# An audio tower on one core: a new order of the same stages on every engine

## The reference

```python
h = layernorm(patches @ tok_W.T + tok_b) * gamma + beta
# attention 0: 16 heads of 64, causal, tanh-capped scores, gated
q, k, v = (layernorm(h) @ w_qkv) split by heads
attn = softmax(causal(50 * tanh(q @ k.T / 8 / 50)))
h = h + ((attn @ v) * sigmoid(layernorm(h) @ w_gates)) @ w_out
# feed-forward 0: three products, then tanh
h = h + tanh(layernorm(h) @ weight @ aux1 @ aux2 + bias)
# attention 1: 16 heads of 16, a sparse (Fenwick) mask
h = h + (softmax(mask(q1 @ k1.T / 4)) @ v1) @ W_proj + b_proj
# feed-forward 1: inputs and weights rounded to blockwise FP4 first
y = fp4(layernorm(h))
h = h + fp4(silu(y @ fp4(w_gate).T) * (y @ fp4(w_up).T)) @ fp4(w_down).T
```

## Time and profile before

| | |
|---|---|
| three runs | 325.51, 326.44, 325.51 us; median 325.51 |
| profiled execution | span 326.4 us, from its first to its last instruction |
| TensorE (matmuls) busy | 303.4 us, 93%, 5142 matmuls |
| VectorE busy | 240.5 us, 74%, 519 instructions |
| ScalarE busy | 121.4 us, 37% |
| mean granted clock of TensorE | 0.989 of 2.4 GHz |

### The profile page before, as it was taken

How to read it: one execution, slowest core, us unless ns; L and a number is a source line. 1 busy time by engine, 2 the same in 40 slices (tenths; PEclk the granted TensorE clock), 3 DMA queues, 4 the chain that set the end, 5 groups by cost and what they waited for, 6 DMA issues and landing times.

```text
span 326.4 us, 11811 instructions
## 1 busy us (share of the span) xinstructions
PE 303.4 (93%) x5142; PEld 265.7 (81%) x5142; DVE 240.5 (74%) x519; ACT 121.4 (37%) x267; POOL 26.1 (8%) x50
## 2 busy tenths in 40 slices
...
DMA packets 8821, 12.80 MB, mean 39 GB/s; under 512 B 826, under 2 KB 5698, under 8 KB 8772
## 3 DMA queue, kind: packets, MB, share of 16 engines
q1 hardware_dynamic: 8772, 12.06, 11.2%
...
## 4 chain that ended last, share of the span: by engine, by line
PE 81%; DVE 10%; DMA 3%; issue 3%; ACT 1%; SPq 1%; POOL 0%; DVEq 0%; ACTq 0%
PE psum L1226 71%; PE psum L1416 2%; DMA ffw_raw<-in_L_ffn_aux_weight_dram 2%; PE psum L1542 2%; PE psum L1438 1%; DMA tokw_raw<-in_L_tok_W_dram 1%; PE psum L1297 1%; PE psum L1322 1%; DVE qs L846 1%; DVE hha L849 1%; DVE qma L1174 1%; PE psum L1253 1%; PE psum L1345 1%; ACT qma L759 1%; PE psum L1519 1%
## 5 line engine op out<-in xcount | busy, mean ns | idle before, releaser
L555 POOL TENSOR_TENSOR ln_rs<-ln_mv,minus_half 128x1 f32<-128x1 f32 x40 | 24.9, 628 | 262.4 <-DVE ln_mv L917 262.4
L1226 PE MATMUL psum<-aT_hi,wqkv_hi 128*128 128x256 f32 x128 | 37.5, 293 | 0.4 <-DVE xT_lo L865 0.2
L1226 PE MATMUL psum<-aT_lo,wqkv_hi 128*128 128x256 f32 x128 | 36.1, 282 | 0.0
L1226 PE MATMUL psum<-aT_hi,wqkv_lo 128*128 128x256 f32 x128 | 35.9, 280 | 0.0
L570 ACT ACTIVATE qkT<-psum 128x512 f32<-128x512 f32 x32 | 18.9, 598 | 36.2 <-PE psum L1226 36.0
L1226 PE MATMUL psum<-wout_s,oT 128*128 128x256 f32 x128 | 29.4, 383 | 0.0
L1226 PEld LDWEIGHTS psum<-wout_s,oT 128*128 128x128 f32 x128 | 23.7, 190 | 3.4
L1226 PEld LDWEIGHTS psum<-aT_hi,wqkv_hi 128*128 128x128 f32 x128 | 24.1, 188 | 1.2 <-issue 0.9
L1226 PEld LDWEIGHTS psum<-aT_lo,wqkv_hi 128*128 128x128 f32 x128 | 24.1, 188 | 0.0
L1226 PEld LDWEIGHTS psum<-aT_hi,wqkv_lo 128*128 128x128 f32 x128 | 24.1, 188 | 0.0
L1226 PE MATMUL psum<-bias_parts,pick_r 128*128 128x256 f32 (+1 forms) x40 | 15.1, 378 | 6.2 <-DVE tokw_lo L865 1.6
...
## 6 DMA issues: line engine op xcount, KB each, us to landing
...
w_raw<-in_L_attn_W_qkv_dram SPq DMA_DIRECT2D x1, 768.0 KB, 10.2
...
```

Of the source, the lines that this page charges most:

```text
L555: nc.gpsimd.tensor_tensor(ln_rs[:, s, k, j:j + 1], ln_mv[:, s, k, j, 1:2], minus_half[:, :], ALU.pow).then_inc(rstd_ready[f"{k}_{j}"], 1)
L1226: return nc.tensor.matmul(o_, a, b, start=first, stop=last)
```

## The change

The five lists of `ORDER` are replaced by five others with the same names. Nothing else in the program changes, but as the banks are given out in the order of TensorE's list, they fall differently too. In TensorE's list 211 of 304 places hold another name than before, in ScalarE's 171 of 223, in VectorE's 317 of 418, in GpSimd's 21 of 41, in SyncE's 4 of 11. The lists were searched anew with a model of the program that also prices a change of TensorE's tile size. The core of the diff (TensorE's head, the middle of pass 2, the end; VectorE's head; SyncE's stores):

```diff
     "pe": """
-        turn_tok xT0.0 bcast warm5 tok0.0 warm3 xT1.0 warm4 tok1.0 warm2 xT0.1 warm1 warm0 turn_ff tok0.1 aT.0
-        join_ff1 xT1.1 qk7.0 qk1.0 tok1.1 qk3.0 v00.0 v01.0 v12.0 qk4.0 qk0.0 qk5.0 v02.0 qk2.0 v11.0 qk6.0
...
-        out0.0 s00.1 s01.1 turn_up1 oT10.0 v01.1 oT11.0 turn_up0 v11.1 v12.1 v02.1 out1.0 v10.1 turn_down
...
-        nT_1.1 xT1.3 bT_0.1 down_1.0 s00.2 s01.2 ffn_1.1 tok1.3 mix00.2 val1_0.1 qk1_0.1 mix01.2 s10.2 bT_1.1
-        mix02.2 s11.2 qk1_1.1 aT.3 sc1_0.1 mix10.2 qk1.3 val1_1.1 qk6.3 v01.3 mix11.2 mx1a_0.1 qk3.3 oT01.2
-        sc1_1.1 mix12.2 mx1b_0.1 v11.3 o1T_0.1 qk5.3 proj_0.1 mx1a_1.1 mx1b_1.1 qk2.3 qk4.3 o1T_1.1 v10.3
...
-        mix10.3 hT0_0.1 oT01.3 oT00.3 hT1_0.1 mix11.3 mix12.3 out0.3 down_0.1 oT11.3 oT10.3 hT0_1.1 nT_1.2
-        ffn_0.2 nT_0.3 hT1_1.1 out1.3 ffn_0.3 bT_0.2 down_1.1 ffn_1.2 bT_0.3 qk1_0.2 val1_0.2 qk1_0.3 nT_1.3
...
-        yT_1.2 g0_0.3 g1_0.3 g0_1.2 g1_1.2 u0_1.2 tail3 u0_0.3 u1_1.2 u1_0.3 hT0_0.2 hT1_0.2 yT_1.3 g0_1.3
-        u0_1.3 g1_1.3 u1_1.3 hT0_1.2 hT1_1.2 down_0.2 hT0_0.3 hT1_0.3 down_1.2 down_0.3 hT0_1.3 hT1_1.3 tail2
-        down_1.3""",
+        turn_tok xT0.0 warm5 warm3 xT1.0 warm4 warm2 warm1 tok0.0 bcast tok1.0 xT0.1 warm0 aT.0 turn_ff tok0.1
+        xT1.1 join_ff1 qk7.0 tok1.1 qk3.0 v00.0 v01.0 qk1.0 v02.0 v12.0 v10.0 qk4.0 qk5.0 qk0.0 qk2.0 v11.0
...
+        turn_gate0 oT00.0 qk3.1 qk4.1 qk5.1 qk2.1 qk6.1 mix10.0 mix11.0 mix12.0 oT01.0 qk7.1 qk1.1 qk0.1 out0.0
+        turn_up1 s00.1 s01.1 turn_up0 oT10.0 v01.1 oT11.0 v11.1 v12.1 v10.1 out1.0 v02.1 turn_down s10.1 s11.1
...
+        down_1.0 s00.2 s01.2 bT_0.1 ffn_1.1 tok1.3 mix00.2 mix01.2 mix02.2 bT_1.1 qk1_0.1 s10.2 s11.2 qk1_1.1
...
+        qk5.3 v11.3 mx1b_0.1 mx1a_1.1 mx1b_1.1 o1T_0.1 qk2.3 proj_0.1 v10.3 o1T_1.1 qk4.3 oT00.2 proj_1.1 qk0.3
...
+        hT1_0.1 nT_0.2 hT0_0.1 out0.3 down_0.1 hT1_1.1 oT11.3 hT0_1.1 nT_1.2 oT10.3 nT_0.3 ffn_0.2 ffn_0.3
+        out1.3 bT_0.2 down_1.1 bT_0.3 qk1_0.2 ffn_1.2 qk1_0.3 nT_1.3 sc1_0.2 bT_1.2 ffn_1.3 val1_0.2 sc1_0.3
...
+        u0_0.2 g1_0.2 yT_0.3 o1T_1.3 u1_0.2 proj_1.3 g0_0.3 g1_0.3 yT_1.2 tail2 u1_0.3 g0_1.2 g1_1.2 u0_1.2
+        tail1 u1_1.2 u0_0.3 yT_1.3 g0_1.3 g1_1.3 hT1_0.2 u1_1.3 hT0_0.2 u0_1.3 hT1_1.2 hT0_1.2 down_0.2 hT0_0.3
+        down_1.2 hT1_0.3 down_0.3 hT0_1.3 hT1_1.3 down_1.3 tail3 tail0""",
...
     "dve": """
-        xT0.0 turn_tok split_tokb split_qkv0 split_qkv1 tokA0.0 tokB0.0 tokC0.0 xT1.0 st1_0.0 split_qkv3
-        tokA1.0 tokB1.0 ln1_0.0 tokC1.0 st1_1.0 xT0.1 split_qkv2 ln1_1.0 tokA0.1 tokB0.1 aT.0 split_b xT1.1
...
+        turn_tok split_tokb xT0.0 tokA0.0 xT1.0 tokB0.0 tokC0.0 st1_0.0 tokA1.0 tokB1.0 split_b ln1_0.0 tokC1.0
+        st1_1.0 split_qkv1 ln1_1.0 xT0.1 split_qkv3 aT.0 tokA0.1 tokB0.1 xT1.1 split_qkv4 tokA1.1 tokB1.1
...
     "sp": """
-        load.2 wout load.3 store_0.0 store_1.0 store_0.1 store_1.1 store_0.2 store_1.2 store_0.3 store_1.3""",
+        load.2 wout load.3 store_0.0 store_1.0 store_1.1 store_0.1 store_0.2 store_0.3 store_1.2 store_1.3""",
```

More of the change, by code:

```diff
@@ L54 @@
[L54 to L58, removed]
```

118 lines of the change are left out of this document (60 added, 58 removed).

## The result

The kernel after takes 329.53 us (median of four runs, 328.77 to 330.91), the one before 325.98 in the same session: a ratio of 1.010, with an interval of 1.006 to 1.014. It is 1.0% slower, where 1% faster was forecast.

What follows compares the result with a forecast made beforehand. TensorE was taken to bound the kernel to some 264 us, VectorE from there to about 309. The sum -1.65 - 1.4 - 0.7 + 0.3 - 0.3 + 0.4 = -3.35 us against 325.51 gave 322.2, range 319.5 to 325.8.

Steps and rivals of the forecast that it cites:

- Part 1: TensorE's tile-size changes, 77 before and 61 after: 0.27 us a pair, together 1.65 us gained (bounds 1.2 and 2.1).
- Part 2: TensorE's 1.54 us instruction wait behind `s11.2` and the half clock after it: 1.4 us gained, bounds 3.2 or nothing.
- instructions late: Longer runs of small matmuls on TensorE starve twice, 1.54 us each, one with slow clock: 328.3 us; chance 0.10.
- Part 3: `turn_up1` covers the 0.68 us wait of `s00.1` for VectorE's addition behind `out0.0`: 0.7 us gained, or 0.
- Part 4: Head, reordered, with `split_b` and `split_qkv1` before `ln1_1.0` on VectorE: 0.3 us lost, bounds 1 gained and 1 lost.
- Part 5: Tail, `ffn_0.3` before `out1.3` to remove VectorE's 1.48 us tanh wait: 0.3 us gained, bounds 0 and 1.5.
- nothing arrives: In VectorE's tail, TensorE's savings become idle time before `sa0`; only 0.3 us stays, 325.2 us; chance 0.13.

Runs made afterwards that it cites:

- the second profile: The kernel before, unchanged, profiled a second time: a span of 323.4 us (325.49 us timed).
- head_fill: The kernel after with `warm0` made of ten fillers instead of one, inside TensorE's wait before `aT.0`: 332.12 us, ratio 1.021 to the kernel before.

## Why the prediction was wrong

- *Part 1, tile size: right in mechanism and nearly in size.* A pair measured 0.21 to 0.29 where 0.27 was taken, so the six pairs that went are an estimated 1.3 to 1.7 us; no run has the price of a change between the two small sizes. TensorE's busy time fell at the same 5142 matmuls, by 0.5 us on the page and not by the 1 to 2 that were to show it, with 13 us more at half clock (20.5 against 7.5), so it neither shows nor refutes the sum. The middle, where most of these changes lie, gained 1.8 us.
- The Trainium skill (TensorEngine Tiling (Array Packing), Key Properties; TensorE: Matmul & The Clock Gate, Step-by-step) has the drain of which the prediction made an estimated 0.05 us a change. That is too little here: 0.10 to 0.15 was measured.
- *Part 2, the wait at 173.6: failed.* Only 1.0 us of it stands in the second profile, and such waits came back as 1.07 inside `mx1a_1.1` with a half clock behind it, and as 1.30 inside `mx1b_1.3`. The 1.4 counted here was not there, as one profile had been taken as typical. The rival "instructions late" had named the very run, two waits and one half clock, and was given 0.10. Its 328.3 lies near the measured 329.53 by luck all the same: the new middle with these waits in it was faster than before, and what made the kernel slower was above all the head, which the rival didn't have.
- The Trainium skill (Runtime: NRT & Kernel Launch, Instruction fetch mechanics) gives blocks of 256 instructions, which the traces bear out, and holds that the pace of issue mostly hides them. Here small matmuls use up a block in under 2 us, and 0.7 to 2 us remain.
- *Part 3, `out0.0`: right, but only half as much was won.* The wait of 0.68 us behind it, in both profiles of before, is gone in all of the new middle's. But all of them have a new one soon after, 0.3 us at `v11.1` for ScalarE's copy of `v_aug`, which both profiles of before lack.
- *Part 4, the head: the step that decided.* 0.3 us of loss was forecast, 4 measured. Two terms failed. The first is the start of `aT.0`, forecast at 21.7 from the durations on VectorE, which came at 23.87. 0.8 of these 2.2 us are the fillers: two of the five ran at half clock (1.07 each and not 0.54) and put `tok0.0` at 12.06, not 11.3. The other 1.4 are VectorE's chain itself, since in `head_fill` `tok0.0` started at 11.29, as forecast, and VectorE's last step before `aT.0` still ended only at 23.00. The prediction doesn't write this sum out, so which of its terms was short stays open. The second is the clock: the longer wait for `aT.0` was priced as time alone, and the half clock behind it, put at nothing, costs 1.8 more. The 4.6 us of stages between `aT.0` and `qk7.0` were right (4.4 at full clock in `head_fill`). Both terms hang on the two splits: moving them gave the 4.1 us back.
- *Part 5, the tail: failed.* The order of TensorE's stages from `g1_1.2` on was compared by what stands last, not by where it would idle. The two waits, 4.1 and 2.5 us, had no work in them since both fillers had gone to the end, "where the addition and the store hide them". Of the 2.0 us lost, 1.0 stands in the stretch with these waits, and there the fillers won 1.7; the other 1.0 comes with the wait for instructions in `mx1b_1.3`. The gain of 0.3 that was counted didn't come.
- The rival "nothing arrives" isn't what happened: between the head and tail of before, the new middle's gain reaches the end (0.996, 0.993 to 0.999).
- The rows came from an execution 2.5 us above the median, and the sum from them was then taken off the median.
